# Moving two groups of setup loads behind the first sequence's broadcast rows in a Mamba, mixture-of-experts and attention kernel

## The chip, the cores and the metric

The kernel runs on one core of a Trainium2 chip. The metric is the device time of one execution in microseconds (us), as the median of several runs. All tiles are float32; products that need more precision are split into a high and a low half by hand.

## What is computed

The input x is 8 sequences of 256 tokens with 128 features. Four blocks follow each other, each of them a residual on a layer norm:

```python
x = x + mamba(layernorm(x))      # in_w, conv of 4 taps, xproj, dt, scan over 256 tokens, out_w
x = x + moe(layernorm(x))        # 8 experts, top 2, inter = up * silu(gate), then w_down[e]
x = x + attention(layernorm(x))  # gated unit: u * (relu(q k / 256)^2 v) W_out
x = x + moe(layernorm(x))        # the same weights again
```

The scan of the Mamba block has 16 states n for each of 256 channels. In every step t it does `new = exp(A*d_t)*state + d_t*B_t[n]*h_t`, and the output sums `new*C_t[n]` over n. B and C are rows of `xpj = conv @ xproj_w`: one number per token and state, the same for all channels.

## The kernel before

Each engine has its own program, and the programs meet at semaphores. What stands in each program, and in which order, is decided by the table `ORDER`: for every kind of step it has a list of numbers, one per instance, `build_plan` sorts all instances by number, and each engine then writes out its own steps in that order. An engine never passes over a step that waits. A tie between numbers is settled by the order of the table's lines.

All DMAs are issued by SyncE (SP) on one queue. Its steps are `setup` (14 kinds of inputs and weights, among them `gate_w` and `up_w`, with `uv_w` and `wo_w` last), `load_down` (the experts' down weights, 1408 KB in three DMAs), `load_x` (sequences 2 to 7 of x, 768 KB), `bc_out`, `rows`, `move` (small copies inside SBUF) and `store`.

The B and C rows reach all 128 partitions through DRAM. ScalarE copies them to the tile `xe` (step `m_xe`, L799), `bc_out` (L512) writes `xe` to the DRAM tensor `bc`, and `rows` reads it back with a broadcast over the partitions into `rows_ring`. This ring has three places, each of which holds the rows of four states (1 MB). So a sequence has four `rows` steps: block 0 for states 0 to 3, block 1 for states 4 to 7, and so on. For the first sequence block 0 is split in two DMAs, one of 256 KB (L528) and one of 768 KB (L531). Block 3 takes the place of block 0 and waits until GpSimd has used the latter's four states (`m_p` at 4).

```python
def rows(arg):
    u, c = arg
    g = u * (NS // CH) + c
    if c == 0:
        sp.wait_ge(s["d_bc"], 16 * (u + 1))      # the write of bc has landed
    ...
        sp.wait_ge(s["m_p"], CH * (g - NCH + 1))
```

The scan of one state goes through these steps. VectorE makes the input `dbx` (L1072, delta*h times the B row) and does the recurrence `scan` (L1086) into one of four `st` tiles. ScalarE makes `dA`, the decay (L831), eleven tiles ahead at most. GpSimd multiplies `st` by the C row (`mulC`, L644), and for the first two sequences TensorE adds the states up (L1374), with small filling matmuls (L1218, L1223) in between. In the first sequence the B rows of states 0 and 1 come from TensorE (L1304, copied at L1069) and need no DMA; the first `dbx` that reads `rows_ring` is that of state 2. VectorE's order in sequence 0 is scan of state 0, `dbx` of state 1, `dbx` of state 2, scan of state 1, `dbx` of state 3, and so on.

From about 67 us on the expert matmuls (gate and up at L1208 to L1210, down at L1438) of 16 blocks of tokens run beside the Mamba steps of the later sequences. The first down matmul waits for `d_down`, and the norm of sequence 2 (`m_stats`, L992) for `d_xs`, the semaphore of `load_x`.

Of the kernel before, what the change touches and what calls it, by code (L numbers as in the profile page):

```python
# [77 lines left out]
    "m_hi": [676, 1875, 6270, 11548, 17996, 24613, 31045, 37643],  # L78
    "m_ph": [843, 2073, 6544, 11954, 18562, 24978, 31451, 38009],
    "diag1": [829],  # L80
    "rows": [1590, 1596, 1602, 2951, 4561, 4567, 5181, 7039, 8615, 9534, 10606, 12685, 14140, 15618, 17008, 19612,
        20963, 22119, 23508, 25790, 27414, 28809, 29914, 32751, 33875, 35043, 36405, 38786, 40262, 41353, 42873,
        45020],
    "lo_in": [606],
# [16 lines left out]
    "split_gate1": [1414],  # L101
    "m_delta": [1553, 4520, 9468, 14988, 21042, 27573, 34053, 40485],
    "t_exp": [1755],
    "load_down": [87],
    "lo_gate1": [1553],
    "m_dt": [1490, 4457, 9405, 14352, 20826, 27510, 33849, 40335],
    "m_mul2": [-33, 330, 7029, 12676, 19241, 25919, 32131, 38552],
# [54 lines left out]
    "lo_rw": [3369],  # L162
    "load_x": [1435],
    "lo_up2": [3730],
    "lo_up3": [4141],
    "m_g": [4725, 6092, 10913, 17718, 24204, 30735, 37120, 43585],
# [1403 lines left out]
```

## Time and profile before

| | |
|---|---|
| median of 3 runs | 611.3 us (610.47 to 612.3) |
| the profiled execution, its own time | 611.06 us |
| its span | 609.3 us |
| TensorE matmul busy | 588.0 us (97%) |
| VectorE busy | 498.4 us (82%) |
| ScalarE busy | 400.5 us (66%) |
| GpSimd busy | 383.9 us (63%) |
| DMA, mean over the span | 75 GB/s |

The busy times are those of one profiled execution, and the span is the time from its first to its last instruction. TensorE's figure takes in the filling matmuls. PE stands for TensorE, PEld for its weight loads, ACT for ScalarE, DVE for VectorE, POOL for GpSimd, SPq for SyncE's queue. The time in which a DMA is issued and the time to its landing are two things: the first occupies SyncE, the second the data.

### The profile page before, as it was taken

The page shows a single profiled execution, that of the slowest core. Times are in us where ns is not written, and L with a number is a line of the kernel's source. Part 1 is how long each engine was busy: PE and PEld are TensorE (multiplying, and loading weights), DVE is VectorE, ACT ScalarE, POOL GpSimd, SP SyncE. Part 2 cuts the span into 40 slices and gives each one's busy share as a digit, 9 for nine tenths or more (in the row PEclk, how much of TensorE's full clock was granted, in tenths as well). Part 3 has the DMA queues.
Part 4 walks back from the last instruction along what each step waited for, and adds up shares of the span by engine and source line. Part 5 has one row for each costly group of instructions (what it writes and reads, how often), then busy time and mean ns, then how long its engine had stood idle before and what let it go on. Part 6 is the DMA issues. An engine that isn't in the chain of part 4 may idle for free.

```text
span 609.3 us, 13178 instructions
## 1 busy us (share of the span) xinstructions
PE 588.0 (97%) x4572; PEld 551.3 (90%) x4572; DVE 498.4 (82%) x1079; ACT 400.5 (66%) x852; POOL 383.9 (63%) x360
## 2 busy tenths in 40 slices
PE   8879999899999999999999999999999999999997
PEld 7633788489999999999999999999999999999997
DVE  5598889878998999999989999899999995454443
ACT  7976675668668786868587858777676732525340
POOL 1278385479886997689878979599757863000000
PEclk9999999989999999999999999999999999999999
DMA  8933213202230212222210231012222000000000
GB/s 281 282 150 130 93 70 115 96 8 86 79 137 18 75 74 83 82 81 72 83 70 24 96 129 69 22 73 79 82 78 77 2 15 12 12 1 15 1 23 9
DMA packets 18466, 45.43 MB, mean 75 GB/s; under 512 B 2847, under 2 KB 13664, under 8 KB 14178
## 3 DMA queue, kind: packets, MB, share of 16 engines
q1 hardware_dynamic: 18402, 44.61, 21.0%
q8 instruction: 36, 0.59, 0.4%
q14 instruction: 28, 0.23, 0.1%
HBM read 40.15 MB, written 1.31 MB: 68 GB/s over the span
## 4 chain that ended last, share of the span: by engine, by line
PE 82%; ACT 6%; DVE 4%; issue 3%; DMA 3%; POOL 1%; SPq 1%; DVEq 0%; ACTq 0%
PE ps L1438 24%; PE ps L1208 15%; PE ps L1209 14%; PE ps L1210 14%; PE ps L1374 3%; ACT dA L831 3%; PE ps L1487 2%; DVE st L1086 2%; DMA at_uv<-uv_w 1%; PE ps L1478 1%; PE ps L1203 1%; PE ps L1499 1%; PE ps L1293 1%; PE ps L1326 1%; POOL st L644 1%
## 5 line engine op out<-in xcount | busy, mean ns | idle before, releaser
L644 POOL TENSOR_TENSOR st<-st,rows_ring 128x512 f32<-128x512 f32 x128 | 164.4, 1289 | 62.1 <-DVE st L1086 58.5
L1438 PE MATMUL ps<-down,inner_ring 128*128 128x128 f32 (+1 forms) x1408 | 174.4, 275 | 0.7 <-DVE X L1171 0.7
L883 ACT ACTIVATE sg<-ps 128x512 f32<-128x512 f32 x176 | 104.7, 596 | 101.9 <-PE ps L1210 82.3
L1438 PEld LDWEIGHTS ps<-down,inner_ring 128*128 128x128 f32 (+1 forms) x1408 | 167.2, 191 | 3.7 <-issue 1.9
L1086 DVE TENSOR_TENSOR_SCAN st<-dA,ps 128x512 f32<-128x512 f32 x128 | 154.8, 1212 | 2.8 <-ACT dA L831 0.3
L1157 DVE TENSOR_TENSOR inner_ring<-sg,ps 128x512 f32<-128x512 f32 x176 | 118.9, 679 | 44.0 <-ACT sg L883 23.5
L657 POOL TENSOR_TENSOR yacc<-yacc,st 128x512 f32<-128x512 f32 x96 | 125.0, 1302 | 5.1
L831 ACT ACTIVATE dA<-delta,A 128x255 f32<-128x255 f32 x256 | 104.8, 495 | 0.2
L1208 PE MATMUL ps<-xhi,up_hi 128*128 128x256 f32 x352 | 102.6, 291 | 0.0
L1209 PE MATMUL ps<-xlo,up_hi 128*128 128x256 f32 x352 | 99.8, 283 | 0.0
L1210 PE MATMUL ps<-xhi,up_lo 128*128 128x256 f32 x352 | 99.8, 283 | 0.0
L1072 DVE TENSOR_TENSOR ps<-ps,rows_ring 128x512 f32<-128x512 f32 x126 | 86.8, 691 | 11.5 <-DMA rows_ring<-bc 7.7
L1208 PE MATMUL ps<-xhi,gate_hi 128*128 128x256 f32 x320 | 92.6, 289 | 0.0
L1171 DVE SCALAR_TENSOR_TENSOR X<-ps,wts,X 128x128 f32<-128x128 f32 x256 | 74.5, 341 | 20.9 <-PE ps L1438 15.4
L1209 PE MATMUL ps<-xlo,gate_hi 128*128 128x256 f32 x320 | 90.8, 284 | 0.0
L1210 PE MATMUL ps<-xhi,gate_lo 128*128 128x256 f32 x320 | 90.7, 284 | 0.0
L1208 PEld LDWEIGHTS ps<-xhi,up_hi 128*128 128x128 f32 x352 | 67.6, 192 | 0.5 <-ACT sg L883 0.4
L1209 PEld LDWEIGHTS ps<-xlo,up_hi 128*128 128x128 f32 x352 | 67.7, 192 | 0.2
L1210 PEld LDWEIGHTS ps<-xhi,up_lo 128*128 128x128 f32 x352 | 67.7, 192 | 0.0
L1209 PEld LDWEIGHTS ps<-xlo,gate_hi 128*128 128x128 f32 x320 | 61.6, 193 | 0.3 <-issue 0.2
L1208 PEld LDWEIGHTS ps<-xhi,gate_hi 128*128 128x128 f32 x320 | 61.6, 192 | 0.3 <-issue 0.2
L1210 PEld LDWEIGHTS ps<-xhi,gate_lo 128*128 128x128 f32 x320 | 61.6, 192 | 0.0
(152 smaller groups left out, 865.4 us busy)
## 6 DMA issues: line engine op xcount, KB each, us to landing
rows_ring<-bc SPq DMA_DIRECT2D x31, 1024.0 KB, 4.8
moved_rows<-inner_ring SPq DMA_DIRECT2D x96, 32.0 KB, 1.9
inner_ring<-gate_w SPq DMA_DIRECT2D x1, 1408.0 KB, 8.0
inner_ring<-up_w SPq DMA_DIRECT2D x1, 1408.0 KB, 10.6
down<-down_w SPq DMA_DIRECT2D x2, 512.0 KB, 10.4
out<-X SPq DMA_DIRECT2D x8, 128.0 KB, 1.8
X<-x SPq DMA_DIRECT2D x1, 768.0 KB, 7.3
rows_ring<-bc SPq DMA_DIRECT2D x1, 768.0 KB, 5.1
```

The lines of the kernel that those rows point to most:

```text
L644: nc.gpsimd.tensor_tensor(st[:, i % NST], st[:, i % NST], row, ALU.mult).then_inc(s["m_p"], 1)
L657: nc.gpsimd.tensor_tensor(yacc[:, u % 2], yacc[:, u % 2], st[:, i % NST], ALU.add).then_inc(s["m_yacc"], 1)
L831: ins = nc.scalar.activation(dA[:, i % NDA, it, 1:], delta[:, u % 2, it, 1:], ACT.Exp, scale=A[:, it, n:n + 1])
L883: nc.scalar.activation(sg[:, k % 2], two(bank_of(q, 2 * j)), ACT.Silu).then_inc(s["f_sg"], 1)
L1072: nc.vector.tensor_tensor(states_in(u, n), dxps, row, ALU.mult).then_inc(s["m_dbx"], 1)
L1086: nc.vector.tensor_tensor_scan(out=st[:, i % NST].rearrange(flat), data0=dA[:, i % NDA].rearrange(flat), data1=states_in(u, n).rearrange(f ...
L1157: nc.vector.tensor_tensor(inner[:, j], sg[:, k % 2], two(bank_of(q, 2 * j + 1)), ALU.mult).then_inc(s["f_in"], 1)
L1171: nc.vector.scalar_tensor_tensor(out=X[:, u, c, :], in0=part, scalar=wts[:, q % 2, c, e:e + 1], in1=X[:, u, c, :], op0=ALU.mult, op1=ALU.a ...
L1208: nc.tensor.matmul(bank, w[0], xv[0], start=start, stop=False)
L1209: nc.tensor.matmul(bank, w[0], xv[1], start=False, stop=False)
L1210: return nc.tensor.matmul(bank, w[1], xv[0], start=False, stop=stop)
L1438: ins = nc.tensor.matmul(bank_of(q, 2 * NP + e)[:, c * H:(c + 1) * H], act_in, down[0:rows, e, n, :], start=n == 0, stop=n == NB - 1)
```

## The change

Two numbers and one tie of the table `ORDER` change. `load_down` goes from 87 to 1614, `load_x` from 1435 to 2957, and the third number of `rows`, which is block 2 of the first sequence, from 1602 to 1620.

```diff
-    "rows": [1590, 1596, 1602, 2951, ...
+    "rows": [1590, 1596, 1620, 2951, ...
-    "load_down": [87],
+    "load_down": [1614],
-    "load_x": [1435],
+    "load_x": [2957],
```

TensorE, VectorE, ScalarE and GpSimd keep their programs. SyncE's program changes at one place, behind the load of `wo` in the setup. Before, these DMAs stood in a row there (a name on the left of the arrow is written, the one on the right is read; the brackets name the semaphores that the issue waits for; L506 is `load_down`, L501 `load_x`):

```order
L498 DMA wo<-wo_w 128x256
L506 DMA down<-down_w 128x8x128 x2
L506 DMA down<-down_w 96x8x128
L512 DMA bc<-xe 32x256 [waits m_xe]
L501 DMA X<-x 128x12x128
L528 DMA rows_ring<-bc 128x512 [waits w_inlo,d_bc]
L531 DMA rows_ring<-bc 128x1536
L531 DMA rows_ring<-bc 128x2048 x2
L531 DMA rows_ring<-bc 128x2048 [waits m_p]
L512 DMA bc<-xe 32x256 [waits m_xe]
```

Now the same part of SyncE's program reads:

```order
L498 DMA wo<-wo_w 128x256
L512 DMA bc<-xe 32x256 [waits m_xe]
L528 DMA rows_ring<-bc 128x512 [waits w_inlo,d_bc]
L531 DMA rows_ring<-bc 128x1536
L531 DMA rows_ring<-bc 128x2048
L506 DMA down<-down_w 128x8x128 x2
L506 DMA down<-down_w 96x8x128
L531 DMA rows_ring<-bc 128x2048
L531 DMA rows_ring<-bc 128x2048 [waits m_p]
L501 DMA X<-x 128x12x128
L512 DMA bc<-xe 32x256 [waits m_xe]
```

The three down loads moved from ahead of the first `bc` write to a place between blocks 1 and 2, and the load of x moved from ahead of block 0 to behind block 3, which waits for `m_p`.

The second place is VectorE's program where it first reads `rows_ring`. It is the same before and after, and shows what stands in line behind that read (d_r0, d_r1 and d_r2 are the semaphores of the three places of the ring):

```order
L1072 TENSOR_TENSOR ps<-ps,b 128x512 [waits m_bc]
L1017 SCALAR_TENSOR_TENSOR m_xlo<-ps,vec,m_xhi 128x256 [waits m_hi]
L1086 SCALAR_TENSOR_TENSOR st<-dA,ps 128x512 [waits m_dbx,m_dA]
L1069 COPY b<-ps 128x256 [waits m_b0,m_dx]
L1072 TENSOR_TENSOR ps<-ps,b 128x512 [waits m_bc]
L1072 TENSOR_TENSOR ps<-ps,rows_ring 128x512 [waits m_scan,d_r0,m_dx]
L1086 SCALAR_TENSOR_TENSOR st<-dA,ps 128x512 [waits m_dbx,m_dA]
```

Nothing moved here: `dbx` of state 2, with its wait for block 0, stands ahead of the scan of state 1 in both programs.

## Rows read from the trace of the kernel before

**Rows 1.** Busy time by stretch: window, its length, busy time (instructions) by engine, clock, DMA share, GB/s.
```profile
62.00:125.00 63.00, 58.91 (x380) 46.66 (x381) 53.63 (x107) 40.63 (x89) 36.14 (x33) 0.99 0.24 86
125.00:300.00 175.00, 174.45 (x1433) 172.40 (x1433) 160.20 (x343) 130.48 (x280) 147.47 (x134) 0.99 0.21 71
```

**Rows 2.** The chain that ended last, at 30 us: start, length, what.
```profile
29.30 0.82 ACT dA L831 x2
30.12 1.22 DVE st L1086
```

**Rows 3.** Timeline of VectorE: start, length, operation [idle before, releaser].
```profile
22.89 0.70 DVE L1072 TENSOR_TENSOR ps<-ps,b 128x512 f32<-128x512 f32 x1
29.51 0.70 DVE L1072 TENSOR_TENSOR ps<-ps,rows_ring 128x512 f32<-128x512 f32 x1 [5.92 <-DMA rows_ring<-bc]
...
43.19 1.26 DVE L1072 TENSOR_TENSOR ps<-ps,rows_ring 128x512 f32<-128x512 f32 x2
...
62.22 0.47 DVE L992 BATCH_NORM_STATS2 m_bn<-X 128x6 f32<-128x128 f32 x2
```

**Rows 4.** Timeline of ScalarE.
```profile
13.57 0.47 ACT L799 ACTIVATE xe<-ps,one_at 128x256 f32<-128x256 f32 x1
...
17.20 0.73 ACT L717 CAST uv_hi<-at_uv 128x640 fp32r<-128x640 f32 x1 [0.53 <-DMA at_uv<-uv_w]
...
23.17 2.49 ACT L831 ACTIVATE dA<-delta,A 128x255 f32<-128x255 f32 x6
...
50.96 0.47 ACT L799 ACTIVATE xe<-ps,one_at 128x256 f32<-128x256 f32 x1 [9.30 <-PE ps L1293]
```

**Rows 5.** Timeline of SyncE: start, time in which it was issuing, DMA.
```profile
8.63 0.48 SPq L498 DMA_DIRECT2D wo<-wo_w  x1
9.15 8.29 SPq L506 DMA_DIRECT2D down<-down_w  x3
17.49 1.21 SPq L512 DMA_DIRECT2D bc<-xe  x1
18.74 0.65 SPq L501 DMA_DIRECT2D X<-x  x1
23.95 0.35 SPq L528 DMA_DIRECT2D rows_ring<-bc  x1
24.34 12.58 SPq L531 DMA_DIRECT2D rows_ring<-bc  x4
```

**Rows 6.** DMAs issued from 0 to 30 us: count, KB each, median us to landing.
```profile
X<-x SPq DMA_DIRECT2D x1, 768.0 KB, 7.3
rows_ring<-bc SPq DMA_DIRECT2D x1, 768.0 KB, 5.1
down<-down_w SPq DMA_DIRECT2D x1, 384.0 KB, 10.3
...
wo<-wo_w SPq DMA_DIRECT2D x1, 128.0 KB, 8.9
...
bc<-xe SPq DMA_DIRECT2D x1, 32.0 KB, 6.4
```

**Rows 7.** The issues of down: shortest, median and longest time, first and last start.
```profile
L506 SPq DMA_DIRECT2D down<-down_w x3: 443/3697/4067, 9.2 to 13.4; - x3
```

**Rows 8.** The block issued between 36 and 37 us, with nothing else under way.
```profile
rows_ring<-bc SPq DMA_DIRECT2D x1, 1024.0 KB, 4.2
```

**Rows 9.** Time to landing of all eight writes of bc.
```profile
DMA to landing us min/median/max: 1.5/1.5/6.4
```

**Rows 10.** The second write of bc, issued at 51.46 us.
```profile
bc<-xe SPq DMA_DIRECT2D x1, 32.0 KB, 3.3
```

**Rows 11.** Timeline of GpSimd.
```profile
22.62 1.68 POOL L573 TENSOR_TENSOR up_lo<-inner_ring,up_hi 128x704 fp32r<-128x704 f32 x1 [7.76 <-ACT up_hi L710]
27.71 1.27 POOL L644 TENSOR_TENSOR st<-st,rows_ring 128x512 f32<-128x512 f32 x1 [3.41 <-DMA rows_ring<-bc]
```

**Rows 12.** The down matmuls between 60 and 100 us: count, ns, first and last start.
```profile
L1438 PE MATMUL ps<-down,inner_ring x68: 272/275/276, 89.3 to 99.8; 128*128 128x128 f32 x48, 96*128 96x128 f32 x20
```

More of the change, by code:

```diff
@@ L80 @@
     "diag1": [829],
-    "rows": [1590, 1596, 1602, 2951, 4561, 4567, 5181, 7039, 8615, 9534, 10606, 12685, 14140, 15618, 17008, 19612,
+    "rows": [1590, 1596, 1620, 2951, 4561, 4567, 5181, 7039, 8615, 9534, 10606, 12685, 14140, 15618, 17008, 19612,
         20963, 22119, 23508, 25790, 27414, 28809, 29914, 32751, 33875, 35043, 36405, 38786, 40262, 41353, 42873,
```

## The prediction, made before the changed kernel was run

> **What bounds the kernel now.** I read the busy times by stretch first. From 125 us on TensorE has work nearly all the time (174.45 of 175 us to 300 us), and from 62 to 125 us 58.91 of 63 [rows 1]. A transfer that ends sooner can hardly shorten that part; what it can do is let it begin sooner. So the question is what sets the time before 62 us, and there I read the timelines. VectorE ends the `dbx` of state 1 at 22.89 + 0.70 = 23.59 us and begins that of state 2 at 29.51: 5.92 us of standing still, released by block 0 of the rows [rows 3]. Everything behind it in VectorE's program stands with it, the scan of state 1 at 30.12 too.
>
> The chain of waits tells another story: at 30.12 it goes back from the scan to ScalarE's `dA` [rows 2]. That scan needs `dA` of state 1 only. ScalarE made the six instructions for states 1 to 3 from 23.17 on, 0.415 us each, so state 1 was ready at 24.00 [rows 4]. The chain took the `dA` that ended last before 30.12, that of a later state. I go by the DMA.
>
> Next, why block 0 is late. `xe` is complete at 13.57 + 0.47 = 14.04 us [rows 4], but SyncE issues the `bc` write at 17.49, since it spends 9.15 to 17.44 issuing the three down loads [rows 5]; two of the three take about 4 us [rows 7]. The write then needs 6.4 us to land (23.9 us), where the median of all eight is 1.5 [rows 6, 9]. It lands just behind the third down load (issued at 13.4, 10.3 to landing, so 23.7 us) [rows 6, 7]. Then the load of x, issued at 18.74, lands at 18.74 + 7.3 = 26.0, and block 0, issued at 23.95 and 24.34, lands at 24.34 + 5.1 = 29.4 [rows 5, 6]. So the wait is made of three parts: SyncE busy for 3.4 us, the write behind 1408 KB of down weights, the rows behind what is left of 768 KB of x.
>
> **The change, part by part.**
>
> *The write of bc.* SyncE is free from 9.1 us on (8.63 + 0.48 [rows 5]) and issues the write when `xe` is there, at about 14.1. What is still ahead of it is the setup up to `wo`, which lands at 8.63 + 8.9 = 17.5 us [rows 5, 6]. Lower bound of its landing: 0.2 us behind the last load ahead, as it is now behind down (23.7 to 23.9), so 17.7. Upper bound: its whole own flight comes after `wo`, by the shorter row 17.5 + 1.5 = 19.0 [rows 9], by the longer one 17.5 + 3.3 = 20.8 [rows 10]. The write's data is only 32 KB and was queued 3.4 us earlier, which is nearest to today's case, so I take 18.0.
>
> *Block 0.* Its larger part is issued 24.34 - 23.95 = 0.39 us after the smaller one. 1 MB on an empty queue took 4.2 us [rows 8]; the larger part took 5.1 with the tail of x ahead of it [rows 6]. So it lands 4.6 to 5.5 us after the write's landing: 18.0 gives 22.6 to 23.5. VectorE asks for it at 23.59. The wait of 5.92 us goes, all of it, with up to 1 us to spare.
>
> *What is late next.* With block 0 there, `dbx` of state 2 begins at 23.6 and the scan of state 1 at about 24.2 instead of 30.12, 5.9 us earlier; its `dA` is ready at 24.00 [rows 4], just in time. After that I shift the later states by 5.9 and look for whoever can't follow.
> - ScalarE: it has finished all of sequence 0's decays at 50.96 - 9.30 = 41.66 us and then stands 9.30 us until TensorE gives it the next sequence's projection [rows 4]. It can follow.
> - GpSimd: its first product waits 3.41 us for the smaller part of block 0 and starts at 27.71. It is busy with `up_lo` till 22.62 + 1.68 = 24.30 and can start there, 3.4 us earlier, not 5.9 [rows 11]. A product takes 1.27 us, less than VectorE's two steps per state (0.70 + 1.22), so this debt of 2.5 us is worked off in about four states, ahead of the point where a scan needs an `st` tile back. I cost it at nothing; if it weren't covered it would be up to 2.5 us.
> - Block 1 stands right behind block 0 before and after, so it keeps its distance.
> - Block 2 now has the down loads ahead of it. Its first reader is the `dbx` of state 8, at 43.19 now, 37.3 then [rows 3]. Issue: SyncE starts on the down loads at about 18.0 + 0.4 + 0.9 = 19.3 and, if they again hold it for 8.3 us, is free at 27.6; its data then has to follow down's. Block 1 lands about 3.1 us behind block 0 (1 MB at the pace of x, 768 KB in 26.0 - 23.7 = 2.3 us), at 26.1. Down's 1408 KB take 4.2 us at that pace and at most the 10.3 us that the last down load needed to land [rows 6]; block 2 itself takes 4.2 [rows 8]. It lands between 34.5 and 40.6. Only the slow end costs something: 40.6 - 37.3 = 3.3 us. I take the fast end, since x has the same pieces of 512 bytes per row as down, and cost it at nothing.
> - Block 3 waits for `m_p` at 4, about 31 us then, and is first read four states after block 2. By the two steps of VectorE per state, 0.70 + 1.22 us [rows 2, 3], that is at least 7.7 us later, at 45 us or after. If it lands 4.2 us behind block 2 [rows 8], it is there at 38.7, and even behind the slow end at 44.8. Behind its wait in SyncE's program stand now the load of x and the second `bc` write.
> - x is issued behind block 3, whose wait ends at about 31 us,, and read at 62.22, then 56.3 [rows 3]; down is read at 89.3, then 83.4 [rows 12]. Both have over 10 us.
> - The second `bc` write stands behind all this in SyncE's queue and is issued at 51.46 now, 45.6 then, when SyncE is idle again.
>
> *Sum.* From there on every engine works by semaphores, nothing by the clock on the wall, so the rest shifts as a whole: 611.06 - 5.9 = 605.2 us against the profiled execution's own time (its span is 609.3). The median of the runs is 0.24 us above that execution, so 605.4 us.
>
> **A rule against part of this.** The rows show 1.5 us for a lone write of bc and 4.2 us for a lone block of 1 MB [rows 8, 9]. The Trainium skill ("DMA: Bandwidth & Descriptors", on the anatomy of one DMA) puts about 2.0 us of fixed cost on each DMA, most of it the receipt of the write, longest when HBM is the target, plus bytes at 436 GB/s; it fitted this on the GpSimd path. If the write paid that in full behind `wo`, it would land at 19.6, the 1 MB at 24.4, 0.8 us past VectorE's need: an estimate by that page of 606.2 us. That is inside the first rival below, whose numbers come from rows alone.
>
> **The rivals.**
> 1. *The wait shrinks, but stays* (20%). The write lands at 19.0 to 20.8, block 0 4.6 to 5.5 us later: 23.6 to 26.3. VectorE's wait is then 0 to 2.7 us, the gain 5.9 down to 3.2. Block 2 at the slow end takes up to 3.3 away at another place. The two don't add up, since a VectorE that is late at state 2 asks later for state 8 as well: 605.9 to 608.7. For it: transfers of these first 30 us land far later than alone. Against: most of that was queueing behind loads that are no longer there.
> 2. *More than that* (8%). ScalarE waits 0.53 us for `uv_w` before 17.20 us [rows 4]. If the setup's last loads land sooner without down data on the same DMA engines, the whole start moves by up to that, and by twice that if the load waited for before it gives as much: 604.9 to 604.3 us.
> 3. *No change* (8%). The chain of waits is right and ScalarE is what VectorE waits for [rows 2], or the later part takes the time back: TensorE stands still 4.1 us between 62 and 125 us [rows 1], and if these pauses are set by something that doesn't move, they grow. Then 610 to 612.5 us. Against it: the `dA` at 24.00, and that I find nothing that doesn't move.
> 4. *Slower* (4%). SyncE is held by the down loads much longer than 8.3 us, because 2 MB of rows are ahead of them, and block 2 is issued late. Nothing else may pass it, block 3 included. It breaks even when block 2 lands at today's need, 43.19 us, 8.7 us past my 34.5; landing at 46 us it would give 611.3 + 2.8 = 614.1. The stall today is 8.3 us in all, so it would have to double.
>
> **How the numbers follow.** The likeliest case (60%) is the wait gone up to a few tenths, a gain of 5.2 to 6.2 us, and its time is 605.4. The range leaves out cases 3 and 4 (12%), the far ends of case 2 (3%) and of case 1 (5%): 604.3 to 608.2. A measurement of this kernel can tell about 0.3%, 1.8 us, from no change. Faster by more than that are the likeliest case, case 1 nearly whole and case 2: 88%. Within it is case 3: 8%. Slower is case 4: 4%.
>
> **What the profile would show.** Right: the `bc` write issued at about 14.1 us and landed at 17.7 to 19; no wait, or one under 0.5 us, in front of the first `dbx` from `rows_ring`, at 23.6; the scan of state 1 at about 24.2; no wait for rows at state 8; the second `xe` at about 45 us instead of 50.96; the first down matmul at 83.4; the same TensorE busy time in a span of about 603.4. Wrong: the write landing after 19, or SyncE's down issues that last beyond 33 us with a DMA wait at state 8, would cut the gain; the scan of state 1 moved but `xe` not would mean that another engine holds sequence 0; and a shift at 62 us that is gone at 125 us would mean that the later part had room that I took for none.

## Result, and the profile after

| | median of runs | lowest to highest | runs | profiled execution, its span, mean clock |
|---|---|---|---|---|
| before | 611.16 us | 610.47 to 612.3 | 4 | 611.06, 609.3, 0.997 |
| changed | 603.19 us | 602.58 to 604.29 | 4 | 603.73, 601.9, 1.000 |

The changed kernel is faster: ratio 0.987, 95% interval 0.9847 to 0.9892, a gain of 8.0 us. The forecast was 605.4 (604.3 to 608.2), so the direction was right and the time lies 1.1 us below the range.

SyncE's timeline of the changed kernel answers to [rows 5]: start, time in which it was issuing, DMA.

```profile
7.64 0.43 SPq L498 DMA_DIRECT2D wo<-wo_w  x1
14.06 0.33 SPq L512 DMA_DIRECT2D bc<-xe  x1
17.65 0.32 SPq L528 DMA_DIRECT2D rows_ring<-bc  x1
18.02 0.91 SPq L531 DMA_DIRECT2D rows_ring<-bc  x2
18.97 7.22 SPq L506 DMA_DIRECT2D down<-down_w  x3
26.23 5.07 SPq L531 DMA_DIRECT2D rows_ring<-bc  x2
31.34 0.43 SPq L501 DMA_DIRECT2D X<-x  x1
45.86 0.32 SPq L512 DMA_DIRECT2D bc<-xe  x1
```

The write of `bc` is issued at 14.06 instead of 17.49. Its reader, L528, starts at 17.65 instead of 23.95, and the second write stands at 45.86 instead of 51.46.

VectorE's timeline answers to [rows 3]:

```profile
21.59 0.70 DVE L1072 TENSOR_TENSOR ps<-ps,b 128x512 f32<-128x512 f32 x1
23.88 0.70 DVE L1072 TENSOR_TENSOR ps<-ps,rows_ring 128x512 f32<-128x512 f32 x1 [1.59 <-DMA rows_ring<-bc]
24.48 1.21 DVE L1086 TENSOR_TENSOR_SCAN st<-dA,ps 128x512 f32<-128x512 f32 x1
...
37.56 1.26 DVE L1072 TENSOR_TENSOR ps<-ps,rows_ring 128x512 f32<-128x512 f32 x2
...
56.35 0.48 DVE L992 BATCH_NORM_STATS2 m_bn<-X 128x6 f32<-128x128 f32 x2
```

Two things are to be seen. The wait for block 0 is 1.59 us where it was 5.92. And the instruction ahead of it starts at 21.59 where it was 22.89: VectorE itself is 1.3 us earlier. ScalarE's timeline, beside [rows 4], shows where that comes from:

```profile
13.56 0.47 ACT L799 ACTIVATE xe<-ps,one_at 128x256 f32<-128x256 f32 x1
15.81 0.20 ACT L715 ACTIVATE rw<-rw_raw 128x8 fp32r<-128x8 f32 x1
15.91 0.72 ACT L717 CAST uv_hi<-at_uv 128x640 fp32r<-128x640 f32 x1
...
21.87 2.49 ACT L831 ACTIVATE dA<-delta,A 128x255 f32<-128x255 f32 x6
...
45.36 0.47 ACT L799 ACTIVATE xe<-ps,one_at 128x256 f32<-128x256 f32 x1 [5.00 <-PE ps L1293]
```

`xe` of the first sequence comes at the same time as before (13.57), but `uv_hi` starts at 15.91 instead of 17.20 and no longer waits for its load. The landings answer to [rows 6] (DMAs issued from 0 to 30 us: count, KB each, median us to landing):

```profile
down<-down_w SPq DMA_DIRECT2D x1, 384.0 KB, 10.1
at_uv<-uv_w SPq DMA_DIRECT2D x1, 320.0 KB, 8.7
...
wo<-wo_w SPq DMA_DIRECT2D x1, 128.0 KB, 8.5
...
bc<-xe SPq DMA_DIRECT2D x1, 32.0 KB, 3.6
```

`wo` is issued at 7.64 and lands at 16.1, not at 17.5.

**The shift over the program.** The third `bc` write starts at 87.62 instead of 93.49, the fourth at 139.51 instead of 146.88: 5.87 us earlier at the one, 7.37 at the other. So the two profiles agree up to about 120 us in a shift of 5.9, and 1.5 us are gained between them later. The windows of the kernel before show the place (length, then busy us (instructions) of PE, PEld, DVE, ACT, POOL, then granted clock, DMA share, GB/s):

```profile
120.00:125.00 5.00, 3.07 (x23) 2.66 (x22) 4.31 (x15) 2.64 (x9) 3.82 (x4) 0.92 0.01 3
125.00:130.00 5.00, 5.00 (x35) 5.00 (x35) 3.59 (x11) 2.50 (x7) 3.26 (x4) 0.74 0.05 13
```

and the same work in the changed kernel, 5 us earlier:

```profile
115.00:120.00 5.00, 3.07 (x25) 2.65 (x24) 4.01 (x11) 2.83 (x8) 4.61 (x5) 1.00 0.01 3
120.00:125.00 5.00, 5.00 (x45) 5.00 (x44) 4.49 (x14) 4.20 (x12) 3.25 (x4) 1.00 0.08 20
```

In the execution of before, TensorE's granted clock fell to its lower level (1.2 instead of 2.4 GHz) from 124.2 to 127.6 us, as 0.92 and 0.74 of the two windows come to, just when work was back behind a stretch with gaps; it did 35 matmuls where the other did 45. The changed kernel's execution passed the same stretch without a fall. Whether that belongs to the change was the first thing to find out.

### The profile page after: what moved, and what is told of

Read it like the earlier page. It is cut to its first block, busy times and chain, and to the rows that moved or that the text cites. A ratio compares the mean times of both kernels' runs of the same rounds, so it can differ in the third digit from the quotient of the medians.

```text
span 601.9 us, 13178 instructions
## 1 busy us (share of the span) xinstructions
PE 585.6 (97%) x4572; PEld 549.8 (91%) x4572; DVE 498.4 (83%) x1079; ACT 400.5 (67%) x852; POOL 384.0 (64%) x360
## 4 chain that ended last, share of the span: by engine, by line
PE 83%; ACT 5%; DVE 4%; DMA 3%; issue 3%; POOL 1%; SPq 0%; DVEq 0%; ACTq 0%
PE ps L1438 24%; PE ps L1208 15%; PE ps L1209 14%; PE ps L1210 14%; PE ps L1374 3%; PE ps L1487 2%; ACT dA L831 2%; DMA rows_ring<-bc 2%; DVE st L1086 2%; PE ps L1203 1%; PE ps L1478 1%; DMA bc<-xe 1%; PE ps L1499 1%; PE ps L1293 1%; PE ps L1326 1%
## 5 line engine op out<-in xcount | busy, mean ns | idle before, releaser
L1171 DVE SCALAR_TENSOR_TENSOR X<-ps,wts,X 128x128 f32<-128x128 f32 x256 | 74.6, 342 | 20.8 <-PE ps L1438 15.4
## 6 DMA issues: line engine op xcount, KB each, us to landing
down<-down_w SPq DMA_DIRECT2D x2, 512.0 KB, 10.1
```

Source lines behind the costliest of these rows:

```text
L1171: nc.vector.scalar_tensor_tensor(out=X[:, u, c, :], in0=part, scalar=wts[:, q % 2, c, e:e + 1], in1=X[:, u, c, :], op0=ALU.mult, op1=ALU.a ...
```

## The experiments

Eight kernels ran in two groups: the two kernels once more, `down_only` and `x_only` in the first, the others in the second. The median of before beside the first group was 610.45 us (609.09 to 611.39, 20 runs), beside the second 609.59 us (608.51 to 612.21, 13 runs). Each ratio is against the runs of its group, and each diff against the changed kernel: what it takes out (-) is the changed kernel's.

**The kernel before once more, unchanged.**

> The kernel before, unchanged, against itself. Ratio 1.000, the interval about +-0.3%. The question is TensorE's granted clock. In the profiled execution of before it was 0.92 from 120 to 125 us and 0.74 from 125 to 130 us, and there the changed kernel gained 1.5 us on top of the 5.87 us it had gained by 62 us. Theory P (the clock fall belongs to this kernel, whose quiet stretch from 115 to 125 us comes at an unlucky moment): most executions show a mean clock of 0.997. Theory C (chance, it comes in either kernel in some executions): a mix of 0.997 and 1.000, in both kernels.

609.81 us (608.01 to 611.96, 12 runs), ratio 0.999 (0.9978 to 1.0002). Its windows:

```profile
32.00:34.00 2.00, 1.72 (x5) 0.96 (x6) 1.87 (x3) 1.97 (x4) 1.31 (x2) 0.83 0.48 201
34.00:36.00 2.00, 2.00 (x5) 0.55 (x3) 1.87 (x3) 1.99 (x6) 1.32 (x2) 0.50 0.01 4
...
125.00:130.00 5.00, 5.00 (x45) 5.00 (x43) 4.49 (x14) 4.19 (x12) 3.25 (x4) 1.00 0.08 20
```

Here the fall began at 33.3 us, behind VectorE's long wait in sequence 0, where TensorE has slack, and not at 124. This profile's fourth `bc` write is at 144.52 and its third at 92.62; the one of before had 146.88 and 93.49. So the two executions of one kernel are 0.87 us apart at the third write and 2.36 at the fourth: the fall at 124 us cost 1.5 us, and one execution of this kernel has it where another has not. Against this profile the changed kernel's first one is earlier by 5.19 us at the first `dbx` from `rows_ring` (29.07 and 23.88), 5.00 us at the third write and 5.01 at the fourth: nothing is gained in between.

**The changed kernel once more, unchanged.**

> The changed kernel, unchanged, for more executions. By the shift between the two traces (5.87 us from 62 to 124 us) the ratio is 0.9904 if clock falls come equally often in both kernels (theory C), and 0.9875 or below if they are a matter of the kernel before alone (theory P). Start: the write of bc issued at 14.06 us, the first dbx from the ring between 22.3 and 24.0 us.

603.10 us (601.93 to 603.84, 4 runs), ratio 0.9877 (0.9862 to 0.9892), span 600.1. The interval leaves out the 0.9904 of theory C, but that doesn't decide for theory P: the 0.9904 was worked out from the shift of 5.87 us, and in this profile the first `dbx` is 6.8 us earlier than in the other of its group (29.07 and 22.25). The mean clock was 0.999 or 1.000 in 4 of the 8 runs of the changed kernel and in 2 of the 45 of the kernel before beside the experiments. So by the mean clock, falls do come more often in the kernel before; but the one at 33 us, which costs nothing that shows, lowers the mean as much as one at 124 us. How often the costly one comes in each kernel stays open.

SyncE and VectorE:

```profile
7.80 0.43 SPq L498 DMA_DIRECT2D wo<-wo_w  x1
14.12 0.33 SPq L512 DMA_DIRECT2D bc<-xe  x1
15.77 0.32 SPq L528 DMA_DIRECT2D rows_ring<-bc  x1
```

```profile
21.65 0.70 DVE L1072 TENSOR_TENSOR ps<-ps,b 128x512 f32<-128x512 f32 x1
22.25 0.69 DVE L1072 TENSOR_TENSOR ps<-ps,rows_ring 128x512 f32<-128x512 f32 x1
```

The write lands by 15.77, at once behind `wo` (7.80 + 7.8 = 15.6), and the wait is gone entirely. VectorE is at `rows_ring` at 22.25, 1.6 us earlier than in the first profile of the same kernel, which is also the difference of their own times (603.73 and 601.93, 1.8 us). The late write of the first profile is thus the exception: `three_parts` and `fill_more`, which issue it in the same way, show it landed by 16.41 and 15.56 as well. In the first profile nothing but one packet moved on the queue from 16.5 to 17.6 us, 0.4 us after `wo` was in. Such a late landing is not the only one: the second write of before took 3.3 us [rows 10], and that of the changed kernel's first profile 3.1 (45.86, its row load at 48.94). Why the first write stood there stays open.

**Only the down loads moved.** The load of x goes back ahead of block 0:

```diff
-    "load_x": [2957],
+    "load_x": [1435],
```

> Only the down loads are moved; the load of x stays between the write of bc and block 0. My account: the write lands at about 17.7 us as in the changed kernel, block 0 has 768 KB of x ahead of it, 2.3 us at the pace seen before, so the first dbx from the ring starts at 25.5 to 26.5 us and the gain up to 62 us is 3.3 to 4.0 us (607 to 608 us). Rival (SyncE's issue time and the write behind down are all of it, the load of x is hidden): the full gain, 5.9 us.

604.89 us (603.61 to 605.7, 5 runs), ratio 0.9908 (0.9893 to 0.9923). The write is issued at 14.75 and landed by 16.51, `uv_hi` doesn't wait, and VectorE waits for block 0, which now stands behind 768 KB of x and is in 7.7 us behind the write (16.88 + 7.3 = 24.2; 5.4 in the changed kernel's second profile):

```profile
22.27 0.70 DVE L1072 TENSOR_TENSOR ps<-ps,b 128x512 f32<-128x512 f32 x1
24.27 0.70 DVE L1072 TENSOR_TENSOR ps<-ps,rows_ring 128x512 f32<-128x512 f32 x1 [1.29 <-DMA rows_ring<-bc]
```

My account had put the `dbx` at 25.5 to 26.5 and the time at 607 to 608 us, so it missed: the write landed 1.2 us before the 17.7 that it counted on. The load of x is not hidden, as the rival had it: it still costs 1.8 us by the medians (604.89 and 603.10).

**Only the load of x moved.**

```diff
-    "load_down": [1614],
+    "load_down": [87],
```

> Only the load of x is moved; the down loads stay ahead of the write of bc. My account: the write still lands at about 23.9 us; block 0 lands 5.5 to 6.2 us behind it as in both kernels, so the gain is 0 to 0.5 us (611 us). Rival (the load of x held block 0 back by what was left of it at 23.95 us, 2.1 us): a gain of about 2 us.

609.29 us (608.2 to 610.6, 8 runs), ratio 0.9982 (0.9971 to 0.9993). ScalarE and VectorE:

```profile
16.52 0.21 ACT L715 ACTIVATE rw<-rw_raw 128x8 fp32r<-128x8 f32 x1 [0.59 <-DMA rw_raw<-router_w]
17.24 0.73 ACT L717 CAST uv_hi<-at_uv 128x640 fp32r<-128x640 f32 x1 [0.51 <-DMA at_uv<-uv_w]
```

```profile
22.93 0.70 DVE L1072 TENSOR_TENSOR ps<-ps,b 128x512 f32<-128x512 f32 x1
29.05 0.70 DVE L1072 TENSOR_TENSOR ps<-ps,rows_ring 128x512 f32<-128x512 f32 x1 [5.42 <-DMA rows_ring<-bc]
```

Both waits of ScalarE are there, 1.1 us together, and the first `dbx` from `rows_ring` stands where `before_again` has it (29.07), as my account said. With the down loads in front, moving x gives 610.45 - 609.29 = 1.16 us by the medians (0.52 against the 609.81 of `before_again`, the same program as before), of which the profiles show nothing at that `dbx`, where moving the down loads alone gave 5.56; the sum, 6.72, is 0.6 short of the 7.35 of both.

**The write first, the bulk directly behind it.** This takes the 3.4 us of SyncE's lateness away and leaves the bytes ahead of block 0:

```diff
-    "load_down": [1614],
+    "load_down": [1431],
...
-    "load_x": [2957],
+    "load_x": [1435],
```

> The write of bc goes ahead of the down loads, but the down loads and x stay ahead of block 0. If the late write (SyncE held by the down loads, the write queued behind their data) was the cause by itself, as the first half of my account read, the gain is the full one, 6 to 8 us. If the 2.2 MB between the write and block 0 are enough to hold block 0 back by themselves, the write lands at 16 to 18 us, block 0 nevertheless at 28 to 30 us as before, and the gain is 0 to 1 us.

610.08 us (608.97 to 610.35, 10 runs), ratio 1.000 (0.9984 to 1.0015).

```profile
14.92 0.33 SPq L512 DMA_DIRECT2D bc<-xe  x1
15.29 3.04 SPq L506 DMA_DIRECT2D down<-down_w  x3
18.38 1.40 SPq L501 DMA_DIRECT2D X<-x  x1
19.90 3.85 SPq L528 DMA_DIRECT2D rows_ring<-bc  x1
23.79 1.38 SPq L531 DMA_DIRECT2D rows_ring<-bc  x3
```

```profile
22.44 0.70 DVE L1072 TENSOR_TENSOR ps<-ps,b 128x512 f32<-128x512 f32 x1
30.34 0.70 DVE L1072 TENSOR_TENSOR ps<-ps,rows_ring 128x512 f32<-128x512 f32 x1 [7.20 <-DMA rows_ring<-bc]
```

The write landed in 1.9 us. But 2176 KB stand ahead of block 0, SyncE is held until 23.8 before it can issue the larger part, and VectorE is later than before. That is the second case of the expectation: an early write alone is worth nothing; what counts is when block 0 is in.

**One of three down loads put back.** 512 KB go behind `wo` again, at the end of the setup:

```diff
                     sp.dma_start(dst, src).then_inc(s[sem], 16)
+                load_down(0, range(1))
...
-            def load_down(_):
-                for k in range(NB):
+            def load_down(_, parts=range(1, NB)):
+                for k in parts:
```

> The changed kernel with one of the three down loads (512 KB) put back behind wo, where its issue holds SyncE for 0.44 us only. Queue theory: uv_w lands later again, so ScalarE waits for it about 0.3 to 0.5 us, and the write of bc has 512 KB ahead of it and lands at 17 to 19 us instead of 15.8; the first dbx from the ring is at 23.5 to 25 us instead of 22.25, and the time is 604 to 606 us. Issue theory (only SyncE's stall mattered): nothing changes, 603 us.

605.77 us (604.87 to 607.16, 4 runs), ratio 0.9941 (0.9923 to 0.9959). In its profile line numbers are one higher:

```profile
9.02 0.45 SPq L507 DMA_DIRECT2D down<-down_w  x1
14.76 0.33 SPq L513 DMA_DIRECT2D bc<-xe  x1
20.19 0.32 SPq L529 DMA_DIRECT2D rows_ring<-bc  x1
```

```profile
17.21 0.73 ACT L718 CAST uv_hi<-at_uv 128x640 fp32r<-128x640 f32 x1 [0.29 <-DMA at_uv<-uv_w]
```

```profile
22.90 0.70 DVE L1073 TENSOR_TENSOR ps<-ps,b 128x512 f32<-128x512 f32 x1
25.97 0.70 DVE L1073 TENSOR_TENSOR ps<-ps,rows_ring 128x512 f32<-128x512 f32 x1 [2.37 <-DMA rows_ring<-bc]
```

SyncE is free here (0.45 us for the issue), and still the write needs 5.4 us: the load ahead of it took 10.1 us and lands at 19.1, the write 1.1 us after it. `wo` too lands at 17.6, as in the kernels with all three down loads there. This tells two causes of before apart, SyncE held by the issues and bytes ahead of the write [rows 5, 6]: the bytes hold it back even where its issue is on time. The expectation had named this case, but its sizes were too small: it had the write at 17 to 19 us and the `dbx` at 23.5 to 25. ScalarE's wait for `uv_w` is back too. By the medians (605.77 and 603.37 for `fill_more` beside it, or 603.10 for the changed kernel) 512 KB in this place cost 2.4 to 2.7 us. The profile is of the slowest of its four runs (607.16 us) and shows 3.7 us at the first `dbx` (25.97 less 22.25): 2.4 of waiting for rows, and 1.25 because VectorE itself is later (22.90 instead of 21.65). `xe` came 0.6 late in this execution (14.26), but that isn't what set it: `uv_hi` starts at 17.21 here and at 17.20 in the profile of before, whose `xe` was at 13.57, since in both it waits for `uv_w`.

**Block 0 in three parts.** The rows of state 2, whose B row VectorE needs first, come by themselves (256 KB), on a semaphore `d_rg` of their own; GpSimd's first two products wait for the second part, `d_rf`:

```diff
-                    first = 2 * T
-                    sp.dma_start(rows_ring[:, 0:first], bc[u, 0:first].partition_broadcast(P)).then_inc(s["d_rf"], 16)
+                    first = 3 * 2 * T
+                    for sem, lo, hi in (("d_rg", 4 * T, 6 * T), ("d_rf", T, 4 * T)):
+                        sp.dma_start(rows_ring[:, lo:hi], bc[u, lo:hi].partition_broadcast(P)).then_inc(s[sem], 16)
...
+                elif i == NB0:
+                    dve.wait_ge(s["d_rg"], 16)
```

> The changed kernel with block 0 read back in three parts in the order of need, without the two B rows that are never read from the ring: rows of state 2 (256 KB), then C of 0, B and C of 1 (384 KB), then state 3 (256 KB). In one profile of the changed kernel VectorE waited 1.59 us for the 1 MB of block 0, in the other not at all. If this wait is there in many executions, the first dbx from the ring is at 22.3 us in the profile and the median falls by 0 to 1.5 us against the changed kernel: 601.7 to 603.2. If it isn't: 603.1.

603.38 us (602.43 to 603.95, 4 runs), ratio 0.9898 (0.9884 to 0.9913). No wait, `dbx` of state 2 at 22.20: the same as in the second profile of the changed kernel (22.25). Where the write lands in time, block 0 is in time whole, and there is nothing for the split to win; it would only have helped in an execution like the first one.

**More filling matmuls for TensorE.** To see whether the falls of the clock can be filled away:

```diff
-                    warm(rot[0] if u else chainps, WARM["out"])
+                    warm(rot[0] if u else chainps, WARM["out"] + 5 * u)
```

> The changed kernel with 5 more filling matmuls behind the second sequence's output product, where TensorE is quiet from about 110 to 118 us. In eight executions of the changed kernel the mean clock was 0.997 four times and 0.999 to 1.000 four times. If the quiet stretch calls the fall, and the filling shortens it, the mean clock is 0.999 or 1.000 in nearly all executions and the median falls by 0.3 to 0.7 us. If the fall comes regardless, the clocks are mixed as before; the filling costs 0 to 0.6 us.

603.37 us (603.05 to 603.96, 4 runs), ratio 0.9901 (0.9886 to 0.9916). The mean clocks of its four executions were 0.997, 0.997, 1.0 and 0.999, and its profile has a fall from 110.9 us. That is the second case of the expectation: no gain, and the falls are not gone. Neither this kernel nor `three_parts` beats the changed one.

**All profiles side by side: the start.** Start of `xe` (ScalarE) and of the `dbx` of state 1 (VectorE) with their distance, start of the `bc` write, start of the row load behind it (so landed by then), and start of the first `dbx` from `rows_ring` with the wait ahead of it, all in us:

| kernel | `xe` | `dbx` of state 1 | distance | write | landed by | first `dbx` from rows [wait] |
|---|---|---|---|---|---|---|
| before | 13.57 | 22.89 | 9.32 | 17.49 | 23.95 | 29.51 [5.92] |
| before, again | 13.84 | 22.74 | 8.90 | 17.31 | 23.48 | 29.07 [5.63] |
| `x_only` | 13.57 | 22.93 | 9.36 | 17.52 | 23.01 | 29.05 [5.42] |
| `early_one` | 14.26 | 22.90 | 8.64 | 14.76 | 20.19 | 25.97 [2.37] |
| `write_first` | 14.42 | 22.44 | 8.02 | 14.92 | 19.90 | 30.34 [7.20] |
| `down_only` | 14.25 | 22.27 | 8.02 | 14.75 | 16.51 | 24.27 [1.29] |
| changed | 13.56 | 21.59 | 8.03 | 14.06 | 17.65 | 23.88 [1.59] |
| changed, again | 13.62 | 21.65 | 8.03 | 14.12 | 15.77 | 22.25 [none] |
| `three_parts` | 13.56 | 21.59 | 8.03 | 14.06 | 16.41 | 22.20 [none] |
| `fill_more` | 13.58 | 21.60 | 8.02 | 14.08 | 15.56 | 22.21 [none] |

(In `write_first` the row load starts at 19.90 because SyncE comes to it only then.) The distance splits the kernels: 8.02 or 8.03 us in all six that issue nothing between `wo` and the write, 8.64 with one down load there, 8.90 to 9.36 with all three. That is ScalarE's waiting for `rw_raw` and `uv_w`. From the start of `uv_hi` to the `dbx` of state 1 it is 5.67 to 5.69 us in all ten profiles, and `uv_hi` starts when both `uv_w` is in and ScalarE has come to it, 2.35 us after the start of `xe`. The distance understates the effect where `xe` is late: a later ScalarE waits less.

**The rest of the program.** From the first `dbx` that reads `rows_ring` to the third `bc` write, and to the execution's own time; where behind 110 us TensorE's clock began a fall (3.4 us each); the median of the runs:

| kernel | first `dbx` | to third write | own time | less first `dbx` | fall behind 110 us | median |
|---|---|---|---|---|---|---|
| before | 29.51 | 63.98 | 611.06 | 581.55 | 124.2 | 611.16 |
| before, again | 29.07 | 63.55 | 608.75 | 579.68 | none | 609.81 |
| `x_only` | 29.05 | 63.56 | 608.74 | 579.69 | none | 609.29 |
| `early_one` | 25.97 | 63.55 | 607.16 | 581.19 | 119.8 | 605.77 |
| `write_first` | 30.34 | 63.55 | 609.99 | 579.65 | none | 610.08 |
| `down_only` | 24.27 | 63.55 | 604.69 | 580.42 | 113.0 | 604.89 |
| changed | 23.88 | 63.74 | 603.73 | 579.85 | none | 603.19 |
| changed, again | 22.25 | 63.58 | 601.93 | 579.68 | none | 603.10 |
| `three_parts` | 22.20 | 63.56 | 603.19 | 580.99 | 117.1 | 603.38 |
| `fill_more` | 22.21 | 63.57 | 603.05 | 580.84 | 110.9 | 603.37 |

This is the finding of the study. The own time of every profiled execution is the start of that one `dbx` plus 579.65 to 579.85 us, and 0.7 to 1.5 us more where the clock fell between 110 and 128 us (in the first profile of before 0.4 besides, already there at the third write). The start of the `dbx` lies between 22.2 and 30.3 us and is all that the orders of DMAs change in these profiles.

## Why the time was missed, and what held

**What held.** Block 0 was what VectorE waited for, and not ScalarE's `dA` as the chain of waits had it [rows 2]: in `write_first` the `dbx` of state 1 is 0.45 us earlier than before and that of state 2 0.83 later, with block 0, and in `early_one` it moves with the rows as well. The later part takes nothing back: what follows the first `dbx` is constant over kernels whose `dbx` differs by 8 us, which excludes the rival of no change. In the first profile the second `xe` came at 45.36 (forecast about 45), the scan of state 1 at 24.48 (about 24.2), and state 8 had no wait for rows (37.56, forecast 37.3). For the down weights, TensorE's matmuls (count, ns, first and last start) began at 83.5, forecast 83.4:

```profile
L1438 PE MATMUL ps<-down,inner_ring x1408: 270/275/377, 83.5 to 598.1; 128*128 128x128 f32 x128, 96*128 96x128 f32 x48
```

The down loads held SyncE for 7.22 us, less than the 8.3 I had allowed. GpSimd's debt cost nothing: its first product ran at 22.96 without a wait.

**The step that failed: "VectorE asks for it at 23.59".** I took VectorE's own start as fixed and only the rows as movable. That start was itself late, since ScalarE waited for the small loads at the end of the setup. `uv_w` landed at 17.1 to 17.3 us (issue plus time to landing) in the four profiles with a down load right behind `wo`: before, before again, `x_only` and `early_one`. In the six without it landed at 14.8 to 16.4. ScalarE is ready for it at 15.9 when `xe` starts at 13.6. In `x_only` it waited 0.59 us for `rw_raw` and 0.51 for `uv_w`, and in the changed kernel, where it waited for neither, VectorE's `dbx` of state 1 starts at 21.59 instead of 22.89: that start moved by 1.3 us, and the `dbx` of state 2 can begin at 22.25.

How much of that comes from the down loads is shown only in part. The times to landing are 9.0 to 9.5 us for `uv_w` with them and 7.7 to 8.7 without, but 9.0 in `write_first` as well, where they are issued only at 15.29. And some of the difference is there before any down load is issued (8.5 us at the earliest): the issue of `up_w`, at 4.1 us, held SyncE for 1.38 to 1.96 us in the four and for 0.61 to 1.30 in the six, so that `uv_w` was issued at 7.57 to 8.14 in the four and at 7.12 to 7.46 in the six. The programs are the same up to there, and why this differs stays open. Before again and `three_parts` are closest in it (`uv_w` issued at 7.57 and 7.46), and there `uv_w` landed at 17.07 and 15.86, 1.2 us apart.

I had this as the second rival, with 8% and 0.5 to 1.0 us, as something that might happen beside the main case. It is a term of the sum: the move takes the down loads away from ahead of the write, and just as much from behind the last loads of the setup.

**The step that was mis-sized: the landing of the write, "17.7 to 20.8, so I take 18.0".** It was built on `wo` landing at 17.5 us, a duration measured with 1408 KB behind it. Without those, `wo` landed at 15.2 to 16.3 us in the changed kernel (twice), `three_parts`, `fill_more` and `down_only`, and the write 0.2 to 0.4 us behind it in four of these profiles (15.6 to 16.5); in the fifth the write was late, at 17.65. (In `write_first` it was 16.6 and 16.8.) What is said above of `uv_w` holds here too: `wo` was also issued earlier, at 7.60 to 7.94 instead of 8.05 to 8.63. That a write lands just behind the last load ahead of it was right, and its own flight was not added on. At the 23.59 of my sum this earlier landing would have given nothing. It does at the real need, 22.25: the two errors hang together and point the same way. Block 0 itself was sized short: without x ahead of it it landed 5.4 to 6.2 us behind the write (changed kernel twice, `fill_more`, `x_only`), where I had 4.6 to 5.5. With the late write this left the 1.59 us of wait in the first profile.

**The sum again.** Between the profiles the first `dbx` from `rows_ring` moved from 29.07 or 29.51 to 22.25, by 6.8 to 7.3 us: the wait of 5.6 to 5.9, ScalarE's 0.9 to 1.3, and up to 0.2 from `xe`. Measured were 6.7 between the medians of the two repeated kernels (609.81 and 603.10), 7.35 against the 20 runs of before beside them, and 8.0 in the first comparison. What exceeds 7.3 there is less than one fall of the clock moves an execution by; with four runs a side its cause isn't shown.

**A hit that is none.** The first profile shows a shift of 5.87 us, the 5.9 forecast. It is made of 1.3 that I hadn't counted, of a wait that shrank by 4.3 instead of 5.9, since this execution's write was late, and of 0.2 in the second sequence (63.98 and 63.74 in the table). Only the repetition showed that. I had also forecast a span of 603.4. It was 601.9: the 1.5 between them is the fall of the clock in the execution of before, against which the sum was made. The time of 605.4 has this in it as well: the same kernel's later medians were 609.6 to 610.5 where the sum began at 611.3.

**The page's rule.** The Trainium skill ("DMA: Bandwidth & Descriptors", on the anatomy of one DMA) gives about 2.0 us of fixed cost, fitted on the GpSimd path, and by it I had estimated 606.2 us. On SyncE's queue the traces come out below that: the first write of 32 KB landed 1.5 to 1.7 us after its issue in three profiles (`fill_more`, the changed kernel again, `down_only`), `wo` ahead of it included, where that page's figures give an estimate of 2.1. For 1024 KB they give an estimate of 4.4, and alone it took 4.2 [rows 8]. The 606.2 missed mostly for another reason: it too started from `wo` landing at 17.5 and a need at 23.59. What the same page says under "Queues, rings and completion order", that a DMA's semaphore increment lands only after every earlier write of that DMA engine, is what the write of `early_one` looks like: 5.4 us for 32 KB, in 1.1 us after a load that took 10.1.

## What to carry to other kernels

A duration to landing that was measured with other data behind it is no property of that DMA: before using it in the new order, ask what shared the DMA engines, behind it too, and look whether any early wait of another engine ends on a load of that stretch. When a move takes bulk data off a queue, list every small load of the same microseconds, not only the one under study; each engine that reads one may start earlier. And take two profiles of each kernel before naming a difference of a microsecond: single executions differed here by 1.5 us at one place and 1.6 at another.

## What the runs showed of the hardware

- 512 KB that were issued behind the last setup load, 5.7 us ahead of a write of 32 KB, went with a landing of that write 5.4 us after its issue, where it was 1.5 to 2.3 without them (3.6 in one profile), and with a kernel time longer by 2.4 to 2.7 us.
- The issue of a load can hold SyncE for very different times: the three down loads took 8.29, 7.22 and 3.04 us, the first one of them 0.44 (the shortest in [rows 7]). In `write_first`, where they began at 15.29 with little on the way, the hold appeared at the next DMAs instead: 1.40 us for x and 3.85 for the smaller part of block 0.
- TensorE's granted clock fell to its lower level for some microseconds in eight of the ten profiles (the last few microseconds of the span aside) of a kernel in which TensorE is busy for 97% of the span (3.4 us, and 6.8 in `write_first`, from 30.9). Two profiles of the same program have the fall at 124 us and at 33 us; at 124 us it cost 1.5 us, at 33 us nothing that shows. Each lay behind a stretch in which TensorE had gaps, but the same stretch of the program passed without one in the changed kernel, twice. What decides it stays open.
